# An attention and FFN sandwich on one core: another order of the first quads

## The chip, the cores and the metric

The kernel runs on one core of one Trainium2 chip. The metric is the device time of one execution in microseconds (us). The kernel before was executed three times: 944.52, 944.43 and 942.95 us, median 944.43. A further execution, under the hardware profiler, took 944.22 us, with a span of 942.4 us; all rows here come from it. The difference of 1.8 us between the two lies outside the first and the last instruction.

## The reference, cut to what matters

Four sequences of 1024 rows with 128 channels go through self-attention with 16 heads of 8 channels. Each head's weights are applied to the whole 128-channel input, and the 16 results are projected back to 128 channels by a 2048x128 matrix. A small mixing FFN follows. Layer norms stand before and after each half.

```python
def _L0_attn_ref(x, weight):
    y = x.reshape(b, t, nh, hs).transpose(0, 2, 1, 3)
    scores = jnp.einsum('bhtk,bhsk->bhts', y, y) / math.sqrt(hs)
    attn = jax.nn.softmax(scores, axis=-1)
    o = jnp.einsum('bhts,bsc->bhtc', attn, x)
    o = o.transpose(0, 2, 1, 3).reshape(b, t, nh * c)
    return o @ weight
...
x = x + _layernorm(_L0_attn_ref(_layernorm(x, axis=-1), L0_attn_weight), axis=-1)
x = x + _layernorm(_L0_ffn_ref(_layernorm(x, axis=-1), ...), axis=-1)
```

## The kernel before

**Steps and quads.** The work is cut into 128 steps. A step j is one head of one row of 512 queries (8 rows, 16 heads). A step has two quads, k = 2j and 2j+1; a quad is four blocks of 128 keys against the 512 queries. One quad passes through five engines:

- `score(k)`, line 552, PE (TensorE): four matmuls into the four banks of `ps_s`. It waits until ACT (ScalarE) has read the quad before it (`weighed`), since there is one `ps_s`, and for the operands `op_s` and `op_t` (ring of four steps, `OP_RING`).
- `weigh(k)`, line 733, ACT: the exponential, 128x2048, into `e_f` (ring of four, so it waits for `split` of quad k-4).
- `cast(k)`, line 409: a DMA from the POOL (GpSimd) queue that rounds `e_f` to float16 in `e_hi`. Quad 0 alone is rounded on DVE (VectorE), `round_first`, line 1074.
- `split_quad(k)`, line 1110, DVE: `e_lo` = `e_f` - `e_hi`. It waits for the cast.
- `products(k)`, lines 571 to 573, PE: twelve matmuls, for each of four blocks y_hi x e_hi, y_hi x e_lo, y_lo x e_hi, summed over the step's two quads in `ps_o`. It waits for `split` of its quad. An even quad also waits for `o_split` of the step two before, which frees its half of `ps_o`.

A step ends with `take_o(j)` (ACT, line 738) and `split_o(j)` (DVE, line 1116), which bring the sum to two float16 tiles; `project(j)` (PE, lines 586 to 588, twelve short matmuls into `ps_r`), `invert(j)` (DVE, line 1122), `scale(j)` (ACT, line 745, four instructions, after which `ps_r` is free for the next `project`), `add(j)` (DVE, line 1132).

**The order.** Each engine runs a program written out by hand, a loop over k; nothing is scheduled by a tool. PE does score(k), then products(k-4) (`LAG` = 4), then in some iterations a projection. `step_at(k, lead)` says which step is projected, inverted, scaled or added in iteration k: steps 0 and 1 in the two iterations lead+2 and lead+3, later ones in every second iteration. PE projects with lead 8, ACT and DVE follow with leads 9 and 10.

**The opening.** Before the loop the input is normalised, and the operands of steps 0 to 3 are made on the chip. Those of step 4 onward come through scratch tensors in DRAM: SP (SyncE) writes `yT` and `shT` to `scr_s` and `scr_t` (lines 291 to 302) and loads them back, `load_s` (line 314) and `load_t` (line 321), four DMAs each. The projection's weights are prepared inside the loop: `weight_columns` and sixteen `weight_base` on DVE (lines 1079 and 1082), `square_weights` on ACT (line 805), `weight_sum` on PE, `weight_scale` (eight tiny instructions, lines 1088 to 1094), `weights_high` (ACT, line 752), `weights_neg` (ACT, line 758), `weights_low` (DVE, line 1100). `turn_ffn_weights` (PE, line 538) turns the FFN's weights. The FFN and the norms of a row, and the normalisation of the next sequence, run in pieces between the quads of later rows.

Of the kernel before, what the change touches and what calls it, by code (L numbers as in the profile page):

```python
# [12 lines left out]
P = 128  # L13
# [9 lines left out]
OP_RING = 4  # L23
SPAN = 42
# [6 lines left out]
def sandwich(nc, x, weight, w_r, w_k, w_v, mu_r, mu_k, out):  # L31
# [22 lines left out]
    with ctx:  # L54
# [63 lines left out]
        o_hi = sb("o_hi", [P, 2, BANK], F16)  # L118
        o_neg = sb("o_neg", [P, 2, BANK], F16)
# [22 lines left out]
        l_mid = sb("l_mid", [P, 2, RB, C], F32)  # L142
# [118 lines left out]
        def op_loaded(j):  # L261

            return 128 * (j // OP_RING + 1 - (j % OP_RING < FIRST))

# [5 lines left out]
        def _(sp):  # L270
# [57 lines left out]
            for j in (FIRST, FIRST + 1):  # L328
                load_t(j)
# [33 lines left out]
        def _(pool):  # L363
# [75 lines left out]
            for k in range(LAST):  # L439
                if 0 < k < QUADS:  # L440
                    cast(k)
# [16 lines left out]
        def _(pe):  # L458
# [97 lines left out]
            def products(k):  # L556
                j, q = k // 2, k % 2
                b, ring = batch_of(j), k % EH_RING
                pe.wait_ge(split, k + 1)
# [9 lines left out]
                for g in range(4):  # L569
# [5 lines left out]
                mm.then_inc(product, 1)  # L575

            def project(j):
# [6 lines left out]
                for i in range(RB):  # L584
                    dst, here = ps_r[:, i * P:(i + 1) * P], slice(i * P, (i + 1) * P)
                    nc.tensor.matmul(dst, o_hi[:, j % 2, here], w_hi[:, j % H, :], start=True, stop=False)  # L586
                    nc.tensor.matmul(dst, o_hi[:, j % 2, here], w_lo[:, j % H, :], start=False, stop=False)  # L587
                    mm = nc.tensor.matmul(dst, o_neg[:, j % 2, here], w_neg[:, j % H, :], start=False, stop=True)  # L588
# [29 lines left out]
            for k in range(LAST):  # L618
                if k < QUADS:
                    score(k)  # L620
# [35 lines left out]
            def last_project(u):  # L656
                pe.wait_ge(l_split, u + 1)
                for i in range(PAIR):
                    here = slice(WIDE * u + i * P, WIDE * u + (i + 1) * P)
                    dst = half_ps("project", u)[:, i * P:(i + 1) * P]  # L660
                    nc.tensor.matmul(dst, o_hi[:, LAST_STEP % 2, here], w_hi[:, H - 1, :], start=True, stop=False)
                    nc.tensor.matmul(dst, o_hi[:, LAST_STEP % 2, here], w_lo[:, H - 1, :], start=False, stop=False)
                    mm = nc.tensor.matmul(dst, o_neg[:, LAST_STEP % 2, here], w_neg[:, H - 1, :], start=False, stop=True)
# [49 lines left out]
        def _(act):  # L713
# [21 lines left out]
            def take_o(j):  # L735
                act.wait_ge(product, 2 * j + 2)
                ge(act, projected, j - 1)
                nc.scalar.activation(o_hi[:, j % 2, :], ps_o[:, j % 2, :], ACT.Copy,  # L738
# [109 lines left out]
            for k in range(LAST):  # L848
# [16 lines left out]
                if k == 8:  # L865
                    weights_high()
                if k == 9:
# [554 lines left out]
```

## Time and profile before

| what | value |
|---|---|
| median of three executions | 944.43 us |
| profiled execution, its own time | 944.22 us |
| its span | 942.4 us |
| PE busy (matmul) | 911.7 us, 97% |
| DVE busy | 863.3 us, 92% |
| ACT busy | 755.6 us, 80% |
| POOL busy | 214.3 us, 23% |
| PE in the chain that ended last | 88% |
| DMA engines busy, POOL's cast queue | 73.7% |
| DMA engines busy, SP's queue | 15.3% |

A busy share is a mean over all stages. A matmul's record is longer than its turn on the engine (a 512-column matmul is recorded with 0.38 us and the next one starts 0.22 us after it), so a busy PE may still have small gaps, and durations in a chain are read from start to start. Idle time of an engine that nobody waits for costs nothing.

### The profile page before, as it was taken

The page shows a single profiled execution, that of the slowest core. Times are in us where ns is not written, and L with a number is a line of the kernel's source. Part 1 is how long each engine was busy: PE and PEld are TensorE (multiplying, and loading weights), DVE is VectorE, ACT ScalarE, POOL GpSimd, SP SyncE. Part 2 cuts the span into 40 slices and gives each one's busy share as a digit, 9 for nine tenths or more (in the row PEclk, how much of TensorE's full clock was granted, in tenths as well). Part 3 has the DMA queues.
Part 4 walks back from the last instruction along what each step waited for, and adds up shares of the span by engine and source line. Part 5 has one row for each costly group of instructions (what it writes and reads, how often), then busy time and mean ns, then how long its engine had stood idle before and what let it go on. Part 6 is the DMA issues. An engine that isn't in the chain of part 4 may idle for free.

```text
span 942.4 us, 17739 instructions
## 1 busy us (share of the span) xinstructions
PE 911.7 (97%) x6057; PEld 441.9 (47%) x6057; DVE 863.3 (92%) x1206; ACT 755.6 (80%) x1052; POOL 214.3 (23%) x345
## 2 busy tenths in 40 slices
PE   4889999999999999999999999999999999999996
PEld 2344444454444444444444454544454444544453
DVE  7888898999899999989989999999989998999976
ACT  7778778788879778888778888888878887788855
POOL 2111322221131412213113333222113131132110
PEclk9999999999999999999999999999999999999998
DMA  8999999999899988999889998999989998899830
GB/s 223 193 207 192 214 194 201 221 199 194 179 182 193 188 176 175 210 189 223 181 180 190 192 189 161 185 222 214 191 179 183 196 187 177 175 184 199 163 67 24
DMA packets 100762, 174.17 MB, mean 185 GB/s; under 512 B 21056, under 2 KB 63424, under 8 KB 100672
## 3 DMA queue, kind: packets, MB, share of 16 engines
q0 software_dynamic: 36720, 133.71, 73.7%
q1 hardware_dynamic: 63952, 39.32, 15.3%
q8 instruction: 49, 0.80, 0.3%
q14 instruction: 41, 0.34, 0.1%
HBM read 28.77 MB, written 10.49 MB: 42 GB/s over the span
## 4 chain that ended last, share of the span: by engine, by line
PE 88%; issue 3%; DVE 3%; DMA 2%; ACT 2%; SPq 1%; POOL 1%; POOLq 0%; DVEq 0%; ACTq 0%
PE ps_o L571 24%; PE ps_o L573 22%; PE ps_o L572 22%; PE ps_s L552 8%; PE ps_r L586 3%; PE ps_r L587 3%; PE ps_r L588 3%; DMA e_hi<-e_f 1%; SPq L314 1%; PE ps_x L603 1%; ACT e_f L733 1%; PE ps_x L613 1%; PE ps_x L609 1%; DMA scr_s<-yT 1%; DMA op_t<-scr_t 1%
## 5 line engine op out<-in xcount | busy, mean ns | idle before, releaser
L1110 DVE TENSOR_TENSOR e_lo<-e_f,e_hi 128x2048 f16<-128x2048 f32 x256 | 585.1, 2287 | 37.3 <-DMA e_hi<-e_f 36.7
L733 ACT ACTIVATE e_f<-ps_s 128x2048 f32<-128x2048 f32 x256 | 481.2, 1880 | 150.7 <-PE ps_s L552 141.3
L571 PE MATMUL ps_o<-e_hi,y_hi 128*128 128x512 f16 x1024 | 391.8, 383 | 0.7 <-DVE e_lo L1110 0.5
L573 PE MATMUL ps_o<-e_hi,y_lo 128*128 128x512 f16 x1024 | 389.2, 380 | 0.0
L572 PE MATMUL ps_o<-e_lo,y_hi 128*128 128x512 f16 x1024 | 389.1, 380 | 0.0
L409 POOL DMA_DIRECT2D e_hi<-e_f x255 | 137.5, 539 | 676.7 <-ACT e_f L733 602.1
L571 PEld LDWEIGHTS ps_o<-e_hi,y_hi 128*128 128x128 f16 x1024 | 99.8, 97 | 149.8 <-issue 50.2
L573 PEld LDWEIGHTS ps_o<-e_hi,y_lo 128*128 128x128 f16 x1024 | 100.4, 98 | 121.6 <-issue 1.2
L745 ACT ACTIVATE part<-ps_r,rden 128x128 f32<-128x128 f32 x508 | 144.3, 374 | 13.0 <-DVE rden L1122 12.7
L572 PEld LDWEIGHTS ps_o<-e_lo,y_hi 128*128 128x128 f16 x1024 | 100.5, 98 | 91.8 <-issue 1.4
L552 PE MATMUL ps_s<-op_t,op_s 32*128 32x512 f16 x1024 | 102.5, 388 | 5.4 <-ACT e_f L733 2.9
L586 PE MATMUL ps_r<-w_hi,o_hi 128*128 128x128 f16 x508 | 91.6, 219 | 2.9 <-ACT part L745 2.9
L1132 DVE TENSOR_TENSOR acc<-acc,part 128x512 f32<-128x512 f32 x119 | 83.2, 699 | 12.0 <-ACT part L745 11.7
L587 PE MATMUL ps_r<-w_lo,o_hi 128*128 128x128 f16 x508 | 91.6, 219 | 0.0
L588 PE MATMUL ps_r<-w_neg,o_neg 128*128 128x128 f16 x508 | 91.6, 219 | 0.0
L1116 DVE SCALAR_TENSOR_TENSOR o_neg<-o_hi,ps_o 128x512 f16<-128x512 f16 x127 | 86.2, 679 | 4.0 <-ACT o_hi L738 4.0
L738 ACT ACTIVATE o_hi<-ps_o 128x512 f16<-128x512 f32 x127 | 75.6, 595 | 2.2 <-PE ps_o L573 1.3
L552 PEld LDWEIGHTS ps_s<-op_t,op_s 32*128 32x128 f16 x1024 | 26.5, 91 | 67.9 <-issue 48.4
L586 PEld LDWEIGHTS ps_r<-w_hi,o_hi 128*128 128x128 f16 x508 | 49.7, 98 | 18.3 <-DVE o_neg L1116 2.5
L587 PEld LDWEIGHTS ps_r<-w_lo,o_hi 128*128 128x128 f16 x508 | 49.7, 98 | 14.7
L588 PEld LDWEIGHTS ps_r<-w_neg,o_neg 128*128 128x128 f16 x508 | 49.7, 98 | 0.0
L1122 DVE RECIPROCAL rden<-ps_r 128x4 f32<-128x4 f32 x127 | 22.6, 178 | 5.5 <-PE ps_r L588 5.5
(228 smaller groups left out, 415.7 us busy)
## 6 DMA issues: line engine op xcount, KB each, us to landing
e_hi<-e_f POOLq DMA_DIRECT2D x255, 512.0 KB, 5.0
op_t<-scr_t SPq DMA_DIRECT2D x496, 32.0 KB, 3.7
op_s<-scr_s SPq DMA_DIRECT2D x496, 16.0 KB, 3.3
scr_s<-yT SPq DMA_DIRECT2D x12, 256.0 KB, 4.6
scr_t<-yT SPq DMA_DIRECT2D x12, 256.0 KB, 4.7
out_dram<-res SPq DMA_DIRECT2D x7, 256.0 KB, 4.6
xs<-in_L_attn_x_dram SPq DMA_DIRECT2D x3, 512.0 KB, 6.5
w_last<-in_L_attn_weight_dram SPq DMA_DIRECT2D x1, 1024.0 KB, 12.3
```

Of the source, the lines that this page charges most:

```text
L409: nc.gpsimd.dma_start(flat(e_hi[:, ring]), flat(e_f[:, k % EF_RING])).then_inc(cast_in[ring], 16)
L552: mm = nc.tensor.matmul(ps_s[:, g, :], op_s[here, slot, q * P:(q + 1) * P], op_t[here, slot, :], start=True, stop=True)
L571: nc.tensor.matmul(dst, y_hi[:, b % 2, s, :], e_hi[:, ring, g, :], start=(q == 0 and g == 0), stop=False)
L572: nc.tensor.matmul(dst, y_hi[:, b % 2, s, :], e_lo[:, ring, g, :], start=False, stop=False)
L573: mm = nc.tensor.matmul(dst, y_lo[:, b % 2, s, :], e_hi[:, ring, g, :], start=False, stop=(q == 1 and g == 3))
L586: nc.tensor.matmul(dst, o_hi[:, j % 2, here], w_hi[:, j % H, :], start=True, stop=False)
L587: nc.tensor.matmul(dst, o_hi[:, j % 2, here], w_lo[:, j % H, :], start=False, stop=False)
L588: mm = nc.tensor.matmul(dst, o_neg[:, j % 2, here], w_neg[:, j % H, :], start=False, stop=True)
L733: nc.scalar.activation(e_f[:, k % EF_RING], ps_s[:], ACT.Exp, scale=1.0 / ROOT).then_inc(weighed, 1)
L745: ins = nc.scalar.activation(part[:, j % 2, i, :], ps_r[:, i * P:(i + 1) * P], ACT.Identity, scale=rden[:, j % 2, i:i + 1])
L1110: dve.tensor_tensor(flat(e_lo[:, ring]), flat(e_f[:, k % EF_RING]), flat(e_hi[:, ring]), ALU.subtract).then_inc(split, 1)
L1116: dve.scalar_tensor_tensor(out=o_neg[:, j % 2, :], in0=o_hi[:, j % 2, :], scalar=2.0 ** O_BITS, in1=ps_o[:, j % 2, :], op0=ALU.mult, op1=A ...
```

## The change

`EARLY`: the first four steps, not the first two, are projected in consecutive iterations, and these are lead+4 to lead+7. `O_RING`: `o_hi` and `o_neg` have four slots, not two. `ROUNDED`: DVE rounds quads 0 and 1, and the DMA cast of quad 1 is gone. `HIGH_FIRST`: in quads 0 to 11 the eight matmuls on `e_hi` come first, on the cast alone, and the four on `e_lo` last, behind `split`. The products of quad 1 are parted around score(5). SP loads s and t of step 4 before s and t of step 5. Weight preparation moves one or two iterations later, the turning of the FFN weights from iteration 12 to 20. ACT does `scale` ahead of `take_o`. `l_mid`, a tile of the last row, now lies in `w_raw`, which is free by then.

```diff
+O_RING = 4
+EARLY = 4
+ROUNDED = 2
+HIGH_FIRST = 12
...
-        l_mid = sb("l_mid", [P, 2, RB, C], F32)
+        l_mid = w_raw[:].rearrange("p (n k) c -> p n k c", n=2)[:, :, 0:RB, :]
...
-            if k in (lead + 2, lead + 3):
-                return k - lead - 2
-            return (k - lead) // 2 if k > lead + 3 and (k - lead) % 2 == 0 else None
+            if lead + EARLY <= k < lead + 2 * EARLY:
+                return k - lead - EARLY
+            return (k - lead) // 2 if k >= lead + 2 * EARLY and (k - lead) % 2 == 0 else None
...
             for j in (FIRST, FIRST + 1):
                 load_s(j)
-            for j in (FIRST, FIRST + 1):
                 load_t(j)
...
-                if 0 < k < QUADS:
+                if ROUNDED <= k < QUADS:
                     cast(k)
...
-            def products(k):
+            def products(k, groups=range(4)):
                 j, q = k // 2, k % 2
                 b, ring = batch_of(j), k % EH_RING
-                pe.wait_ge(split, k + 1)
+                if k >= HIGH_FIRST:
+                    pe.wait_ge(split, k + 1)
+                elif k < ROUNDED:
+                    pe.wait_ge(rounded, k + 1)
+                else:
+                    pe.wait_ge(cast_in[ring], cast_count(k))
...
+                if k < HIGH_FIRST:
+                    for g in range(4) if groups[0] == 0 else ():
+                        s = 2 * g + q
+                        nc.tensor.matmul(dst, y_hi[:, b % 2, s, :], e_hi[:, ring, g, :], start=(q == 0 and g == 0), stop=False)
+                        nc.tensor.matmul(dst, y_lo[:, b % 2, s, :], e_hi[:, ring, g, :], start=False, stop=False)
+                    if groups[-1] == 3:
+                        pe.wait_ge(split, k + 1)
+                        for g in range(4):
+                            mm = nc.tensor.matmul(dst, y_hi[:, b % 2, 2 * g + q, :], e_lo[:, ring, g, :], start=False,
+                                                  stop=(q == 1 and g == 3))
+                        mm.then_inc(product, 1)
+                    return
...
             for k in range(LAST):
+                if k == LAG + 1:
+                    products(1, range(2))
                 if k < QUADS:
                     score(k)
...
-                if 1 <= k - LAG < QUADS:
+                if k == LAG + 1:
+                    products(1, range(2, 4))
+                if 2 <= k - LAG < QUADS:
                     products(k - LAG)
...
-                if k == 12:
+                if k == 20:
                     turn_ffn_weights()
...
-                ge(act, projected, j - 1)
+                ge(act, projected, j - O_RING + 1)
...
-                if k == 8:
+                if k == 9:
                     weights_high()
-                if k == 9:
+                if k == 10:
                     weights_neg()
...
                 if k == 2:
+                    round_quad(1)
+                if k == 3:
                     weight_columns()
...
-                if k == 6:
+                if k == 7:
                     weight_scale()
-                if k == 8:
+                if k == 10:
                     weights_low()
```

The order on PE from score(4) to score(6), before (lines of the kernel before; 552 is the score, 571 to 573 the products):

```order
L552 MATMUL ps_s<-op_t,op_s 128x512 [waits weighed,first_t_in,first_s_in]
L552 MATMUL ps_s<-op_t,op_s 128x512 x3
L552 MATMUL ps_s<-op_t,op_s 128x512 [waits weighed]
L552 MATMUL ps_s<-op_t,op_s 128x512 x3
L571 MATMUL ps_o<-e_hi,y_hi 128x512 [waits split]
L572 MATMUL ps_o<-e_lo,y_hi 128x512
L573 MATMUL ps_o<-e_hi,y_lo 128x512
```

and with the change (559 is the score, 584 and 585 the products on `e_hi`, 589 those on `e_lo`):

```order
L559 MATMUL ps_s<-op_t,op_s 128x512 [waits weighed,first_t_in,first_s_in]
L559 MATMUL ps_s<-op_t,op_s 128x512 x3
L584 MATMUL ps_o<-e_hi,y_hi 128x512 [waits rounded]
L585 MATMUL ps_o<-e_hi,y_lo 128x512
L559 MATMUL ps_s<-op_t,op_s 128x512 [waits weighed]
L559 MATMUL ps_s<-op_t,op_s 128x512 x3
L589 MATMUL ps_o<-e_lo,y_hi 128x512 [waits split,rounded]
L589 MATMUL ps_o<-e_lo,y_hi 128x512 x3
```

The eight products of quad 1 on `e_hi` (the pair of rows comes four times) now stand between score(4) and score(5) and wait for a rounding on DVE; the four on `e_lo` follow score(5).

The order on DVE from the first `split_quad` on, before (1110 is `split_quad`, 1079 and 1082 the weights' columns and bases):

```order
L1110 TENSOR_TENSOR e_lo<-e_f,e_hi 128x2048 [waits rounded]
L1079 TENSOR_TENSOR w_col<-w_raw,w_last 128x16 [waits w_last_in,w_in]
L1082 SCALAR_TENSOR_TENSOR xs<-w_raw,w_col,w_last 128x127 [waits dve_step]
L1082 SCALAR_TENSOR_TENSOR xs<-w_raw,w_col,w_last 128x127 x7
L1110 TENSOR_TENSOR e_lo<-e_f,e_hi 128x2048 [waits cast_in_1]
L1082 SCALAR_TENSOR_TENSOR xs<-w_raw,w_col,w_last 128x127 x4
L1110 TENSOR_TENSOR e_lo<-e_f,e_hi 128x2048 [waits cast_in_2]
```

and with the change (1139 is `split_quad`, 1103 `round_quad`, 1108 and 1111 the columns and bases):

```order
L1139 TENSOR_TENSOR e_lo<-e_f,e_hi 128x2048 [waits rounded]
L1103 CAST e_hi<-e_f 128x2048 [waits weighed]
L1139 TENSOR_TENSOR e_lo<-e_f,e_hi 128x2048 [waits rounded]
L1108 TENSOR_TENSOR w_col<-w_raw,w_last 128x16 [waits w_last_in,w_in]
L1111 SCALAR_TENSOR_TENSOR xs<-w_raw,w_col,w_last 128x127 [waits dve_step]
L1111 SCALAR_TENSOR_TENSOR xs<-w_raw,w_col,w_last 128x127 x7
L1139 TENSOR_TENSOR e_lo<-e_f,e_hi 128x2048 [waits cast_in_2]
L1111 SCALAR_TENSOR_TENSOR xs<-w_raw,w_col,w_last 128x127 x4
```

The rounding of quad 1 is new on DVE, and the split of quad 1 now stands ahead of the weights' columns and bases and waits for no DMA.

## Rows read from the trace of the kernel before

**Rows 1.** Waits of PE from 20 to 75 us: in total, times, longest

```profile
PE ps_r L586 <- ACT part L745: 2.9, 2, 2.2
PE ps_s L552 <- DMA op_t<-scr_t: 2.2, 1, 2.2
PE ps_s L552 <- ACT e_f L733: 2.0, 1, 2.0
```

**Rows 2.** Waits of PE from 75 to 915 us

```profile
PE ps_o L571 <- DVE o_neg L1116: 0.2, 1, 0.2
```

**Rows 3.** Timeline of PE: start, duration, line and operation [idle before, releaser]

```profile
26.92 0.40 PE L552 MATMUL ps_s<-op_t,op_s 32*128 32x512 f16 x4 [1.98 <-ACT e_f L733]
...
43.71 0.39 PE L552 MATMUL ps_s<-op_t,op_s 32*128 32x512 f16 x4
...
46.73 0.39 PE L552 MATMUL ps_s<-op_t,op_s 32*128 32x512 f16 x4
...
50.42 0.39 PE L552 MATMUL ps_s<-op_t,op_s 32*128 32x512 f16 x4
...
57.82 0.49 PE L538 MATMUL ps_x<-ident,wf 128*128 128x128 f32 x3
...
74.75 0.39 PE L552 MATMUL ps_s<-op_t,op_s 32*128 32x512 f16 x4
```

**Rows 4.** A stretch: from and to, length, busy PE, PEld, DVE, ACT, POOL (instructions), PEclk, DMA share, GB/s

```profile
39.60:42.90 3.30, 3.30 (x10) 1.13 (x9) 3.07 (x2) 3.30 (x2) 0.53 (x1) 0.51 0.53 111
```

**Rows 5.** Timeline of ACT

```profile
27.37 1.88 ACT L733 ACTIVATE e_f<-ps_s 128x2048 f32<-128x2048 f32 x1 [0.50 <-PE ps_s L552]
29.14 1.90 ACT L805 ACTIVATE w_neg<-w_raw 128x2048 f16<-128x2048 f32 x1
...
31.03 1.87 ACT L733 ACTIVATE e_f<-ps_s 128x2048 f32<-128x2048 f32 x1
...
33.81 0.59 ACT L738 ACTIVATE o_hi<-ps_o 128x512 f16<-128x512 f32 x1
...
41.22 1.98 ACT L752 ACTIVATE w_hi<-xs,ws 128x2032 f16<-128x2032 f32 x1
...
52.84 1.14 ACT L745 ACTIVATE part<-ps_r,rden 128x128 f32<-128x128 f32 x4
```

**Rows 6.** Timeline of DVE

```profile
14.15 1.23 DVE L1074 CAST e_hi<-e_f 128x2048 f16<-128x2048 f32 x1
...
18.19 2.28 DVE L1110 TENSOR_TENSOR e_lo<-e_f,e_hi 128x2048 f16<-128x2048 f32 x1
20.39 0.19 DVE L1079 TENSOR_TENSOR w_col<-w_raw,w_last 128x16 f32<-128x16 f32 x1
20.62 2.18 DVE L1082 SCALAR_TENSOR_TENSOR xs<-w_raw,w_col,w_last 128x127 f32<-128x127 f32 x8
...
36.14 0.15 DVE L1088 TENSOR_SCALAR w_bits<-w_sum 128x1 f32<-128x1 f32 x1
...
37.58 0.69 DVE L1116 SCALAR_TENSOR_TENSOR o_neg<-o_hi,ps_o 128x512 f16<-128x512 f16 x1
...
43.23 2.34 DVE L1100 SCALAR_TENSOR_TENSOR w_lo<-xs,ws,w_hi 128x2032 f16<-128x2032 f32 x1 [0.56 <-ACT w_hi L752]
```

**Rows 7.** Timeline of POOL's and SP's DMA issues

```profile
17.60 0.78 POOL L409 DMA_DIRECT2D e_hi<-e_f  x1 [1.31 <-ACT e_f L733]
20.28 0.53 POOL L409 DMA_DIRECT2D e_hi<-e_f  x1 [1.91 <-ACT e_f L733]
...
24.27 7.10 SPq L314 DMA_DIRECT2D op_s<-scr_s  x8
31.42 6.42 SPq L321 DMA_DIRECT2D op_t<-scr_t  x8
```

**Rows 8.** DMA issue at 17.60 us: size, us to landing

```profile
e_hi<-e_f POOLq DMA_DIRECT2D x1, 512.0 KB, 6.4
```

**Rows 9.** DMA queues over the span: packets, MB, share of the 16 engines

```profile
q0 software_dynamic: 36720, 133.71, 73.7%
```

More of the change, by code:

```diff
@@ L568, in products @@
                 dst = ps_o[:, j % 2, :]
-                for g in range(4):
+                if k < HIGH_FIRST:
[10 more added lines that the diff above has]
+                    return
+                for g in groups:
                     s = 2 * g + q
@@ L736, in take_o @@
                 act.wait_ge(product, 2 * j + 2)
-                ge(act, projected, j - 1)
-                nc.scalar.activation(o_hi[:, j % 2, :], ps_o[:, j % 2, :], ACT.Copy,
+                ge(act, projected, j - O_RING + 1)
+                nc.scalar.activation(o_hi[:, j % O_RING, :], ps_o[:, j % 2, :], ACT.Copy,
                                      scale=2.0 ** -O_BITS).then_inc(taken, 1)
@@ L864, in _ @@
                     keep_weight_sum()
-                if k == 8:
+                if k == 9:
                     weights_high()
-                if k == 9:
+                if k == 10:
                     weights_neg()
-                if k == 12:
+                if k == 20:
                     turn_in_ffn_weights()
+                j = step_at(k, LAG + 5)
+                if j is not None and j < LAST_STEP - 1:
+                    scale(j)
                 j = (k - LAG - 2) // 2
@@ L873, in _ @@
                     take_o(j)
-                j = step_at(k, LAG + 5)
-                if j is not None and j < LAST_STEP - 1:
-                    scale(j)
                 for r, o in rows_at(k):
@@ L892, in last_take @@
                 act.wait_ge(projected, LAST_STEP - 1)
-                nc.scalar.activation(o_hi[:, LAST_STEP % 2, :], ps_o[:, LAST_STEP % 2, :], ACT.Copy,
+                nc.scalar.activation(o_hi[:, LAST_STEP % O_RING, :], ps_o[:, LAST_STEP % 2, :], ACT.Copy,
                                      scale=2.0 ** -O_BITS).then_inc(l_taken, 1)
@@ L1114, in split_o @@
                 dve.wait_ge(taken, j + 1)
-                ge(dve, projected, j - 1)
-                dve.scalar_tensor_tensor(out=o_neg[:, j % 2, :], in0=o_hi[:, j % 2, :], scalar=2.0 ** O_BITS,
+                ge(dve, projected, j - O_RING + 1)
+                dve.scalar_tensor_tensor(out=o_neg[:, j % O_RING, :], in0=o_hi[:, j % O_RING, :], scalar=2.0 ** O_BITS,
                                          in1=ps_o[:, j % 2, :], op0=ALU.mult, op1=ALU.subtract).then_inc(o_split, 1)
@@ L1288, in last_split @@
                 dve.wait_ge(projected, LAST_STEP - 1)
-                dve.scalar_tensor_tensor(out=o_neg[:, LAST_STEP % 2, wide(u)], in0=o_hi[:, LAST_STEP % 2, wide(u)],
+                dve.scalar_tensor_tensor(out=o_neg[:, LAST_STEP % O_RING, wide(u)], in0=o_hi[:, LAST_STEP % O_RING, wide(u)],
                                          scalar=2.0 ** O_BITS, in1=ps_o[:, LAST_STEP % 2, wide(u)], op0=ALU.mult,
```

39 lines of the change are left out of this document (21 added, 18 removed).

## The prediction

> **What bounds the kernel now.** I read the waits of PE first. From 75 to 915 us PE, the engine of the matmuls, waits for 0.2 us in all [rows 2]: the middle is PE's own work, and a start that is x us earlier ends x us earlier. Two quads and a projection take 3.02 and 3.69 us from score to score (43.71 to 46.73 to 50.42) [rows 3], 6.71 together. From 20 to 75 us PE waits 7.1 us in the rows shown: 2.0 for the exponential before score(5), 2.2 for the operand `op_t` of score(8), 2.9 in two waits for `scale` before projections [rows 1]. From 39.60 to 42.90 us the granted clock is 0.51, thus 1.2 GHz in place of 2.4, though PE is busy throughout; that cost 3.3 x 0.49 = 1.6 us [rows 4]. The change touches this stretch and nothing behind it but `l_mid`, which only changes an address. So the sum is the start of score(17): 74.75 us before [rows 3]. By then five projections have run in both kernels.
>
> **The units.** Start to start, a weighing takes 1.77 (27.37 to 29.14), the next score can start after about 1.93 (its record of 1.88 and a hand-over), and a weighing starts 0.45 after its score (26.92 to 27.37) [rows 3, 5]. A score and its products hold PE 3.02, the score 0.33 of it; a projection 0.7. On ACT: squares or `weights_neg` 1.85, `weights_high` 1.9, `take_o` 0.5, `scale` 1.14, so that with its hand-over the next projection can start some 1.28 after scale's start [rows 5]. On DVE: split 2.2, rounding 1.23, columns 0.23, eight bases 2.1 (four: 1.05), the weight scale 37.58 - 36.14 = 1.45, `split_o` 0.6, `weights_low` 2.25 [rows 6]; for two batch sums I allow 0.4.
>
> **DVE with the change.** The first split starts at 18.19 as before; the rounding of quad 1 follows at 20.4 and its split ends at 23.85, columns and bases at 26.2. Split(2) needs cast(2), issued at 20.28. In the trace the first cast took 6.4 us to land [rows 8]; cast(2) now stands first in its queue, so I take 6.4 again, 26.7. Lower bound 2.7, the bare work of a cast (73.7% of 942.4 us over 255 casts [rows 9]); then the bases at 26.2 set the split. Upper bound 9.1, as if 2.7 more still stood ahead of it. From 26.7: split(2) to 28.9, bases 29.95, split(3) 32.15, bases 33.2, split(4) 35.4, split_o(0) 36.0, split(5) 38.2, weight scale 39.65, split(6) 41.85, split_o(1) 42.45, split(7) 44.65, split(8) 46.85, `weights_low` 49.1, split_o(2) 49.7, split(9) 51.9, split(10) 54.1, sums 54.5, split_o(3) 55.1, invert(0) 55.3.
>
> **PE and ACT with the change.** Score(5) starts at 26.92 as before, because weigh(4) sets it. But the eight products of quad 1 now fill the 2 us ahead of it; the four on `e_lo` end at 28.1. Score(6) then waits for weigh(5) alone, 27.37 + 1.93 = 29.3. ACT does weigh(5), the squares and weigh(6) at 31.03, unchanged [rows 5], so score(7) comes at 32.95. Weigh(7) starts at 33.4, products(3) end at 36.0.
> Score(8) follows at 36.0 if `op_t` of step 4 is there. SP issued its eight s loads from 24.27 and the eight t loads from 31.42 to 37.84 [rows 7]. Now t of step 4 is issued after four s loads, from about 28 to 31.5 us; before, its last DMA left at about 34.6, halfway through the eight, and score(8) came at about 39.1 (43.71 - 3.02 - 1.6). So it arrives about 3 us earlier, at 36.0 or before. The wait of 2.2 us goes, and I take the slow clock to go with it.
> Score(9) 39.05, weigh(9) 39.5. Then ACT becomes the slow one: `weights_high` 41.25, weigh(10) 43.1, `weights_neg` 44.9, take_o(2) 46.7, weigh(11) 47.2. PE: score(10) 42.05, score(11) 45.2, products(7) end 48.15, score(12) waits for weigh(11) until 49.1. Products(8) need split_o(2), 49.8. They end at 52.4; project(0) has its weights (49.1) and ends at 53.15; score(13) 53.2, before at 61.3 (74.75 less two pairs of 6.71). So 8 us are gained here. The four projections in a row give part back: each waits for the scale of the step before, and scale follows a weighing on ACT, a round of 0.75 + 0.45 + 1.77 + 1.28 = 4.25 us against PE's own 3.69. Scale(0) at 55.4, project(1) 56.7, and then 60.95, 65.2 and 69.45; score(17) at 70.2. That is 4.55 earlier. The turning of the FFN weights, in a wait before (57.82 [rows 3]), now stands in PE's full stretch: 0.4 lost. **Gain 4.15 us**, 944.22 - 4.15 = 940.1. The profiled execution is 0.2 below the median of 944.43.
>
> **Edits that I cost at nothing.** Products on `e_hi` first, in quads 2 to 11: in the chain above each split is done before the four late matmuls and nearly always before the first, so only quad 1 profits; cover gone, it would save up to a split of 2.2 us once. The same matmuls in another order, each with its own weight load: no count changes. `O_RING` = 4: it lets `take_o` run ahead of late projections; without it take_o(2) would wait for project(0). The missing cast(1): 2.7 us of the DMA engines; it shows only in the landing of cast(2). DMA load: casts 2 to 9 are issued from 20.3 to 41.4, 8 x 2.7 = 21.6 us of work plus an estimated 4 of loads and scratch writes, done by about 46; cast(9) is needed at 49.7, so they fit, by an estimated 1 to 4 us each.
> POOL's cast of 17.60 lasted 0.78 us, that of 20.28 0.53 [rows 7]; the longer one began while DVE was on its copies for the shift. A rounding on DVE will now run at 20.4, right behind the issue of cast(2). I give this nothing beyond the landing of 6.4. The Trainium skill, "SBUF — State Buffer", section "SBUF: two separate sides", warns against just this: an fp32 copy on VectorE locks GpSimd out while it should write the descriptors of its DMA. By that rule cast(2) would land up to one rounding, 1.2 us, later; the sum would give 941.0 or so. The row of 0.78 fits it, by 0.25 us only.
>
> **The rivals.**
> *More gain, 936 to 938.5.* If scale keeps up, its four waits of 0.56 go, and DVE's 0.5 us behind cast(2) with them: 940.1 - 2.7 = 937.4. For it: after 75 us PE has 0.2 us of waits [rows 2]. Against: there one projection per two quads leaves room; here four come in a row. Chance 0.13.
> *Late casts, 942.* If casts 6 to 8 land 2 us later than taken, DVE, without slack from split(2) to split_o(2), passes it on through products(8): 942.1. For it: more and larger transfers start in 20 to 41 us than PE's waits for the operand suggest there is room for [rows 1]. Against: the sum of work above. Chance 0.13, half of it within 0.2% of no change.
> *One fall of the clock, 941.7.* PE still waits about 1 us before score(6) and before score(12). Before, the 0.51 came behind the wait of 2.2 us [rows 1, 4]; one fall costs 1.6. Chance 0.06. The Trainium skill, "TensorE: Matmul & The Clock Gate", section "Part 1: The HAM clock gate", says that idleness throttles the array; the trace agrees at 39.6.
> *Slower, by the clock.* The same at every new pause (before scores 6, 7 and 12 and in the row of projections, 1 us or less each): four falls cost 6.4, 946.5. It decides from four on; with three the time is 944.9. Against: the longest new pause is half of the 2.2 us. Chance 0.04.
> *It does not do what it says.* If `op_t` of step 4 comes no earlier, because t must wait for the shift's scratch write, score(8) stays at 39.1 and little is left: 943.5 to 944.4. Against: the write is issued ahead of all these loads, and the s loads alone take until 28 [rows 7]. Chance 0.04.
>
> **The numbers.** Forecast 940.1, chance 0.60, own range 938.5 to 941.8. The range is 936.9 to 942.9, which takes in more gain and late casts. A measurement can tell 0.2%, 1.9 us, from no change: faster means below 942.5. Faster: 0.60 + 0.13 + half of 0.13 + 0.06 = 0.85. Same: the other half and the last rival, 0.11. Slower: 0.04.
>
> **What would show it.** In the profile after: score(8) near 36 us without a wait for `op_t`; granted clock 1.0 from 23 us on; score(12) near 49 behind an exponential; project(1) to (4) each waiting about 0.5 us for `part`; score(17) near 70.2; no wait of PE from 75 to 910 us. It is wrong if DVE waits for casts 6 to 8, if a fall of the clock appears after 23 us, or if score(17) comes at 72 or later.

## The result and the profile after

The changed kernel took 940.17 us (median of 7 executions, 938.80 to 941.35), the kernel before, on the same chip and in turn with it, 943.65 us (7 executions, 942.95 to 944.52). The ratio is 0.996, 95% interval 0.9949 to 0.9971: faster by 0.4%, twice what a measurement can tell. The profiled execution took 939.56 us with a span of 937.8 us, 4.66 us less than before's 944.22. PE is busy for 908.8 us, DVE 864.3, ACT 756.1, POOL 212.9; the shares are as before, so the time must be read from the opening.

The waits of PE from 20 to 72 us in the kernel after (in total, times, longest), to be held against [rows 1]:

```profile
PE ps_s L559 <- ACT e_f L762: 2.2, 3, 1.1
PE ps_r L611 <- ACT part L774: 1.7, 4, 0.4
PE ps_s L559 <- issue: 0.7, 1, 0.7
PE ps_o L584 <- DVE o_neg L1145: 0.6, 2, 0.4
```

The wait for `op_t` is gone. The two waits for `part`, one of them 2.2 us long, are now four of 0.4. The waits for an exponential are shorter and more: 1.1 before score(6), 0.4 before score(7), 0.7 before score(12).

The timeline of PE, to be held against [rows 3] (start, duration, line, operation [idle before, releaser]); L559 is the score, L584 a product on `e_hi`, L589 one on `e_lo`, L595 the first kind of product from quad 12 on:

```profile
26.85 0.39 PE L559 MATMUL ps_s<-op_t,op_s 32*128 32x512 f16 x4
27.18 1.04 PE L589 MATMUL ps_o<-e_lo,y_hi 128*128 128x512 f16 x4
29.32 0.40 PE L559 MATMUL ps_s<-op_t,op_s 32*128 32x512 f16 x4 [1.11 <-ACT e_f L762]
...
35.91 0.40 PE L559 MATMUL ps_s<-op_t,op_s 32*128 32x512 f16 x4
...
49.10 0.40 PE L559 MATMUL ps_s<-op_t,op_s 32*128 32x512 f16 x4 [0.70 <-ACT e_f L762]
...
49.87 0.38 PE L584 MATMUL ps_o<-e_hi,y_hi 128*128 128x512 f16 x1 [0.37 <-DVE o_neg L1145]
...
53.22 0.39 PE L559 MATMUL ps_s<-op_t,op_s 32*128 32x512 f16 x4
...
70.28 0.40 PE L559 MATMUL ps_s<-op_t,op_s 32*128 32x512 f16 x4
...
405.90 0.38 PE L595 MATMUL ps_o<-e_hi,y_hi 128*128 128x512 f16 x1 [0.76 <-DVE o_neg L1145]
...
895.89 0.40 PE L559 MATMUL ps_s<-op_t,op_s 32*128 32x512 f16 x4
```

These are score(5), the late products of quad 1, score(6), score(8), score(12), products(8), score(13), score(17), a product near 406 us, and the last score. Beside the forecast:

| start of score | before | forecast | after |
|---|---|---|---|
| 5 | 26.92 | 26.92 | 26.85 |
| 6 | | 29.3 | 29.32 |
| 8 | 39.00 | 36.0 | 35.91 |
| 10 | 46.73 | 42.05 | 41.96 |
| 12 | 54.89 | 49.1 | 49.10 |
| 13 | 61.32 | 53.2 | 53.22 |
| 17 | 74.75 | 70.2 | 70.28 |

Scores 14, 15 and 16 start at 57.49, 61.75 and 66.02, a round of 4.27 us where 4.25 was worked out. The gain is 8.1 us at score(13) and 4.5 at score(17).

The windows of after (from and to, length, busy PE, PEld, DVE, ACT, POOL, PEclk, DMA share, GB/s), the first to be held against [rows 4], and then the second window in the kernel before:

```profile
39.60:42.90 3.30, 3.03 (x18) 1.17 (x16) 3.30 (x3) 3.30 (x2) 0.53 (x1) 1.00 1.00 195
928.00:933.00 5.00, 2.70 (x18) 2.02 (x16) 4.11 (x15) 3.76 (x10) 0.00 (x0) 1.00 0.18 52
```

```profile
928.00:933.00 5.00, 3.26 (x12) 2.52 (x13) 3.35 (x9) 4.01 (x11) 0.00 (x0) 0.75 0.00 0
```

From 39.60 to 42.90 the granted clock is now 1.00 where it was 0.51. From 928 to 933 it is 1.00 where it was 0.75.

**Where the 4.66 us are.** At score(17) the gain is 4.47. Turning the FFN weights costs 0.34 of it (score(20) to score(21) takes 4.03 us where that pair of quads takes 3.69), which leaves 4.13. The last score came at 899.42 us in the timeline of before and comes at 895.89 now: 3.53, so 0.6 is lost on the way. The wait of 0.76 us at 405.90 accounts for it: just ahead of it the gain is 4.35 us (a score at 404.74 that stood at 409.09; before had lost 0.2 in its own wait [rows 2]), behind it 3.53 (409.70 against 413.23). The last score to the end of the span takes 41.91 us where it took 42.98. These 1.07 us come from a stretch in which the change moves only the address of `l_mid`, and in which the clock fell once where it fell twice before. In all fourteen traces the tail takes 41.63 to 41.91 us with one fall in it (eight of them, runs 3 and 6 with the old `l_mid` too) and 42.75 to 43.69 with two (six). So what goes with the longer tail is the second fall, not `l_mid`. The medians, 3.5 us apart, fit the 3.53 of the last score.

The wait at 405.90 is for `o_neg` from DVE. DVE's timeline of after (before: [rows 6]) has, besides quad 1's rounding and split(2), the split which was late there:

```profile
20.32 1.22 DVE L1103 CAST e_hi<-e_f 128x2048 f16<-128x2048 f32 x1
...
26.65 2.29 DVE L1139 TENSOR_TENSOR e_lo<-e_f,e_hi 128x2048 f16<-128x2048 f32 x1 [0.46 <-DMA e_hi<-e_f]
...
49.05 0.68 DVE L1145 SCALAR_TENSOR_TENSOR o_neg<-o_hi,ps_o 128x512 f16<-128x512 f16 x1
...
398.67 2.29 DVE L1139 TENSOR_TENSOR e_lo<-e_f,e_hi 128x2048 f16<-128x2048 f32 x1 [1.60 <-DMA e_hi<-e_f]
```

The split at 398.67 waited 1.60 us for a cast to land; before, the longest such wait near it was 0.67 us, at 401.59. DVE had not made this up by 405.90. The DMA share around it is the same in both traces (1.06 from 390 to 400 us), so why this cast was later is open. The changed kernel's second trace (run 9) has a wait for `o_neg` of only 0.3 us between 390 and 420 us, so its size is not a property of the kernel.

The issues of POOL and SP in after, against [rows 7], and then the landing of cast(2), against [rows 8]:

```profile
20.20 1.47 POOL L416 DMA_DIRECT2D e_hi<-e_f  x1 [3.99 <-ACT e_f L762]
...
21.42 3.81 SPq L322 DMA_DIRECT2D op_s<-scr_s  x4
25.28 3.30 SPq L329 DMA_DIRECT2D op_t<-scr_t  x4
```

```profile
e_hi<-e_f POOLq DMA_DIRECT2D x1, 512.0 KB, 6.4
```

Cast(2) landed in 6.4 us, as taken. Its record on POOL was 1.47 us long instead of 0.53. SP's loads began at 21.42, 2.9 us earlier than before, which was not forecast. What SP waited for ahead of its s loads reads, from 18 to 34 us, first before, then after:

```profile
SPq L309 <- DMA scr_s<-yT: 3.0, 1, 3.0
```

```profile
SPq L317 <- DMA scr_s<-yT: 0.2, 1, 0.2
```

It is the last of the scratch writes of `yT` to `scr_s`: issued at 18.23 before, it landed 6.0 us later; without cast(1) beside it, issued at 18.15, it landed in 3.2 us. The shift's write to `scr_t`, which only the t loads need, landed in 3.2 us instead of 7.7 (issued at 20.83 and 20.92); in neither of the two kernels did SP have to wait for it, since the s loads took longer.

### The profile page after: what moved, and what is told of

Read it like the earlier page. It is cut to its first block, busy times and chain, and to the rows that moved or that the text cites. A ratio compares the mean times of both kernels' runs of the same rounds, so it can differ in the third digit from the quotient of the medians.

```text
span 937.8 us, 17735 instructions
## 1 busy us (share of the span) xinstructions
PE 908.8 (97%) x6057; PEld 439.8 (47%) x6057; DVE 864.3 (92%) x1207; ACT 756.1 (81%) x1052; POOL 212.9 (23%) x344
## 4 chain that ended last, share of the span: by engine, by line
PE 88%; DVE 5%; issue 2%; ACT 2%; DMA 2%; POOL 0%; POOLq 0%; DVEq 0%; ACTq 0%
PE ps_o L595 24%; PE ps_o L597 22%; PE ps_o L596 22%; PE ps_s L559 8%; PE ps_r L611 3%; PE ps_r L612 3%; PE ps_r L613 3%; DVE e_lo L1139 2%; DMA e_hi<-e_f 2%; ACT e_f L762 1%; PE ps_x L628 1%; PE ps_x L638 1%; PE ps_x L634 1%; ACT part L774 0%; PE ps_x L623 0%
## 5 line engine op out<-in xcount | busy, mean ns | idle before, releaser
L595 PE MATMUL ps_o<-e_hi,y_hi 128*128 128x512 f16 x976 | 372.3, 381 | 0.8 <-DVE o_neg L1145 0.8
L597 PE MATMUL ps_o<-e_hi,y_lo 128*128 128x512 f16 x976 | 369.9, 379 | 0.0
L596 PE MATMUL ps_o<-e_lo,y_hi 128*128 128x512 f16 x976 | 369.9, 379 | 0.0
L595 PEld LDWEIGHTS ps_o<-e_hi,y_hi 128*128 128x128 f16 x976 | 94.9, 97 | 142.0 <-issue 46.4
L597 PEld LDWEIGHTS ps_o<-e_hi,y_lo 128*128 128x128 f16 x976 | 95.5, 98 | 115.3
L596 PEld LDWEIGHTS ps_o<-e_lo,y_hi 128*128 128x128 f16 x976 | 95.6, 98 | 86.9 <-issue 0.3
L559 PE MATMUL ps_s<-op_t,op_s 32*128 32x512 f16 x1024 | 102.6, 388 | 4.3 <-ACT e_f L762 3.1
L559 PEld LDWEIGHTS ps_s<-op_t,op_s 32*128 32x128 f16 x1024 | 26.5, 91 | 67.0 <-issue 49.8
L1151 DVE RECIPROCAL rden<-ps_r 128x4 f32<-128x4 f32 x127 | 22.3, 175 | 5.2 <-PE ps_r L613 5.2
```

Source lines behind the costliest of these rows:

```text
L559: mm = nc.tensor.matmul(ps_s[:, g, :], op_s[here, slot, q * P:(q + 1) * P], op_t[here, slot, :], start=True, stop=True)
L595: nc.tensor.matmul(dst, y_hi[:, b % 2, s, :], e_hi[:, ring, g, :], start=(q == 0 and g == 0), stop=False)
L596: nc.tensor.matmul(dst, y_hi[:, b % 2, s, :], e_lo[:, ring, g, :], start=False, stop=False)
L597: mm = nc.tensor.matmul(dst, y_lo[:, b % 2, s, :], e_hi[:, ring, g, :], start=False, stop=(q == 1 and g == 3))
```

## The experiments

The open questions were which of the edits bring the 4.5 us at score(17), whether the slow stretch hung on the wait for `op_t`, whether the longer record on POOL costs anything, and what the row of four late projections gives back. Each run was compared with the kernel before on the same chip; its median was 943.36 us beside the first four, 944.28 beside the next four and 943.09 beside the last four. The changed kernel is 3.5 us faster than it in the result and 3.1 in run 9, so between groups a difference of medians is good to some tenths of a us only, and the starts of the scores say more.

**1. Products in the old order.** In the changed kernel:

```
-HIGH_FIRST = 12
+HIGH_FIRST = 0
```

> The changed kernel with HIGH_FIRST = 0: in quads 2 to 11 the twelve products go back to the old order and wait for the split; quad 1 stays parted around score(5), now six and six. Theory (the splits are always done before PE comes to the products): no difference from the changed kernel, 940.2, within 0.5 us, score(17) again at 70.3 us in the trace. Rival (products that start on the rounded values alone are what lets PE start earlier): 1.5 us or more slower than the changed kernel, with waits of PE for e_lo.

Measured 941.04 us, ratio 0.997 (0.996 to 0.9979). PE's timeline, score(4) and score(17):

```profile
24.75 0.40 PE L559 MATMUL ps_s<-op_t,op_s 32*128 32x512 f16 x4 [0.29 <-issue]
...
70.55 0.39 PE L559 MATMUL ps_s<-op_t,op_s 32*128 32x512 f16 x4
```

Both are 0.28 us later than in after (24.47 and 70.28), so from one to the other the two kernels run alike, and no product waits for `e_lo`. Products on `e_hi` first are worth nothing here. The 0.9 us between the medians do not come from the opening: the last score starts at 896.01 us against 895.89 in after, and of the 2.0 us between the two profiled executions 1.8 lie in the tail, where the clock fell twice in this run.

**2. Quad 1 cast by DMA again.** In the changed kernel, with the weights' columns and bases back in their earlier iterations:

```
-ROUNDED = 2
+ROUNDED = 1
...
-                if k == 2:
-                    round_quad(1)
-                if k == 3:
+                if k == 2:
                     weight_columns()
```

> The changed kernel with quad 1 rounded by the DMA again (ROUNDED = 1) and the weights' columns and bases back in iterations 2 to 4 on DVE. Theory (DVE's chain up to split_o(2) sets products(8)): the rounding costs DVE 1.2 us but saves 2.3 us of waits for casts, so split_o(2) ends at 50.4, not 49.7, and score(17) comes 0.7 us later: 940.9. SP's loads of step 4 start at 24.3 again, not 21.4, and still arrive by 36. Rival (the cast taken from the DMA engines is the main gain, through earlier operands and casts): 2.5 us or more slower than the changed kernel, 942.7, with a wait for op_t at score(8).

Measured 941.1 us, ratio 0.9973 (0.9964 to 0.9983). Score(17) starts at 71.66, 1.4 us later than in after, where 0.7 was expected. At score(13) it is 1.0 us (54.18 against 53.22), which split_o(2) explains; the rest comes at score(14), which waits 0.37 us for `op_t` in this run and not at all in after. The timeline of DVE shows quad 1's split behind its cast, and split_o(2) later than the 49.05 of after:

```profile
24.20 2.29 DVE L1139 TENSOR_TENSOR e_lo<-e_f,e_hi 128x2048 f16<-128x2048 f32 x1 [1.35 <-DMA e_hi<-e_f]
...
50.00 0.68 DVE L1145 SCALAR_TENSOR_TENSOR o_neg<-o_hi,ps_o 128x512 f16<-128x512 f16 x1
```

The rounding on DVE more than pays for itself: it takes 1.2 us of DVE's time, but without it a split waits 1.35 us for the cast, and PE waits twice for `op_t` (0.30 us ahead of score(10), 0.37 ahead of score(14)).

**3. The load order alone.** In the kernel before:

```
             for j in (FIRST, FIRST + 1):
                 load_s(j)
-            for j in (FIRST, FIRST + 1):
                 load_t(j)
```

> The kernel before with one edit: SP issues s4, t4, s5, t5 in place of s4, s5, t4, t5. Theory (each cure of the operand wait works, but the early projections take back most of it): the wait of 2.15 us at score(8) goes, score(10) comes 3.4 us earlier, and then products(6) wait for split_o(1), which stands behind weights_low on DVE; 1.5 us faster than before in the end, 942.1. If the clock falls in that wait instead, 943.6. Rival (the operand wait and its slow clock are worth their full 3.8 us): 939.9.

Measured 941.59 us, ratio 0.9979 (0.997 to 0.9989). PE's timeline, score(8) and score(17), and its wait for `o_neg` from 20 to 72 us:

```profile
36.92 0.40 PE L551 MATMUL ps_s<-op_t,op_s 32*128 32x512 f16 x4
...
73.50 0.40 PE L551 MATMUL ps_s<-op_t,op_s 32*128 32x512 f16 x4
```

```profile
PE ps_o L570 <- DVE o_neg L1115: 2.4, 2, 1.2
```

Score(8) no longer waits, as forecast. But a new wait of 2.4 us for `o_neg` takes the place of the old one: what was late next is DVE, whose weights stand ahead of `split_o`. At score(17) 1.25 of the 2.1 us won at score(8) are left.

**4. The rounding alone.** In the kernel before, `cast(1)` is left to DVE, which rounds quad 1 ahead of the weights' columns:

```
-                if 0 < k < QUADS:
+                if 1 < k < QUADS:
                     cast(k)
...
                 if k == 2:
+                    round_quad(1)
                     weight_columns()
```

> The kernel before with one edit: quad 1 rounded on DVE (in iteration 2, ahead of the weights' columns) and its cast taken from the DMA queue; order of SP's loads unchanged. Theory (removing the cast lets the scratch writes land 3 us earlier, so SP starts at 21.4 and t of step 4 arrives by 36 even in the old order): the same as the edit of the load order, 1.5 us faster than before, 942.1, no wait for op_t at score(8). Rival (only the load order cures the wait): op_t is waited for at score(8) as before and the time is 943.7 or, with 1.2 us more on DVE, 944.5.

Measured 941.64 us, ratio 0.9981 (0.9971 to 0.9992). The issues of SP's loads in this run and, in PE's timeline, score(8):

```profile
21.90 5.97 SPq L314 DMA_DIRECT2D op_s<-scr_s  x8
27.91 6.00 SPq L321 DMA_DIRECT2D op_t<-scr_t  x8
```

```profile
37.58 0.40 PE L552 MATMUL ps_s<-op_t,op_s 32*128 32x512 f16 x4
```

The loads keep their old order and still start at 21.90 instead of 24.27, and score(8) doesn't wait for `op_t`. So the wait had two cures, and the change applies both: the order of the loads, and one cast fewer among the transfers ahead of them. Each alone brings about 1.8 us (943.36 less 941.59 and 941.64), and run 5, which has both, brings 1.6: they do not add up. This run also moved the slow stretch (see the section on the hardware).

**5. Projections, ring and weights as before.** In the changed kernel:

```
-O_RING = 4
-EARLY = 4
+O_RING = 2
+EARLY = 2
...
-                if k == 9:
+                if k == 8:
                     weights_high()
-                if k == 10:
+                if k == 9:
                     weights_neg()
...
-                if k == 7:
+                if k == 6:
                     weight_scale()
-                if k == 10:
+                if k == 8:
                     weights_low()
```

with the turning at 12 and `take_o` ahead of `scale`, as before.

> The changed kernel with EARLY = 2, O_RING = 2, and the weights, the turning of the FFN weights and the order of take_o and scale as before; the opening (rounding, load order, high first, quad 1 parted) is kept. Theory: products(6) wait about 2 us for split_o(1) behind weights_low, score(12) at 52.7, score(13) at 59.2 against 53.2 in the changed kernel and 61.3 before; in the end 2.2 us faster than before, 941.4, so the later projections are worth the other 1.3 to 2. Rival (the opening alone is the gain): as the changed kernel, 940.2.

Measured 942.72 us, ratio 0.9986 (0.9975 to 0.9998). Its timeline of PE, scores 12, 13 and 17, and its waits from 20 to 72 us:

```profile
52.72 0.39 PE L559 MATMUL ps_s<-op_t,op_s 32*128 32x512 f16 x4
...
59.16 0.39 PE L559 MATMUL ps_s<-op_t,op_s 32*128 32x512 f16 x4
...
74.28 0.40 PE L559 MATMUL ps_s<-op_t,op_s 32*128 32x512 f16 x4
```

```profile
PE ps_r L611 <- ACT part L774: 2.9, 2, 2.3
PE ps_o L584 <- DVE o_neg L1145: 2.3, 2, 1.2
```

Scores 12 and 13 were expected at 52.7 and 59.2. The wait of 2.3 us for `part` and that for `o_neg` are back. So later projections with a deeper ring, and weights that keep out of the way of `split_o`, carry somewhat more than half. Against the kernel before on its own chip this run is 1.6 us faster and the change 3.5, which leaves 1.9 for them. At score(13) they are worth 5.9 us; at score(17) 4.0, of which 1.7 are the slow stretch between scores 13 and 14 of this run (see the section on the hardware), so 2.3. What each of these edits is worth by itself was not run.

**6. PE kept busy in the wait for `op_t`.** In the kernel before, ten matmuls of 512 columns, whose product nobody reads, stand ahead of score(8):

```
+            def fill(n):
+                pe.wait_ge(w_summed, 1)
+                for _ in range(n):
+                    nc.tensor.matmul(ps_x[:], ident16[:], y_hi[:, 0, 0:RB, :]...,
+                                     start=True, stop=True)
...
+                if k == 8:
+                    fill(10)
```

> The kernel before with ten matmuls of 512 columns into the idle ps_x ahead of score(8), where PE waits 2.15 us for op_t; the wait is filled, not shortened, and the results do not change. Theory (the stretch at half the clock comes from that pause): granted clock 1.0 from 37 to 43 us, score(9) 3.0 us after score(8) in place of 4.7, 1.6 us faster than before, 942.0. Rival (the fall has another cause, or its loss is hidden by ACT): the same as before, 943.65.

This failed: 946.19 us, ratio 1.0025 (1.0009 to 1.0041), slower. PE's timeline and two windows of this run:

```profile
36.64 2.32 PE L620 MATMUL ps_x<-y_hi,ident 128*128 128x512 f16 x10
...
39.25 0.39 PE L552 MATMUL ps_s<-op_t,op_s 32*128 32x512 f16 x4 [0.29 <-DMA op_t<-scr_t]
...
60.05 0.22 PE L586 MATMUL ps_r<-w_hi,o_hi 128*128 128x128 f16 x1 [2.25 <-ACT part L753]
...
60.82 0.39 PE L552 MATMUL ps_s<-op_t,op_s 32*128 32x512 f16 x4
...
65.53 0.39 PE L552 MATMUL ps_s<-op_t,op_s 32*128 32x512 f16 x4
```

```profile
39.60:42.90 3.30, 3.30 (x22) 1.35 (x19) 3.04 (x2) 3.20 (x2) 0.53 (x1) 1.00 0.50 103
60.80:65.50 4.70, 4.70 (x18) 1.59 (x16) 4.58 (x7) 2.91 (x5) 0.53 (x1) 0.64 0.57 146
```

The clock does stay at 1.00 from 39.60 to 42.90, as expected. But score(13) starts at 60.82, only 0.5 us ahead of before's 61.32. Counted from score(8), which came 0.25 us later here, 0.75 us are won: of the 1.7 us which the slow stretch cost PE (4.71 us from score(8) to score(9) where it is 3.02 here), 0.9 were hidden behind other engines that were late anyway; score(10) now waits 0.49 us for its exponential. And the clock falls in the quad behind score(13) instead, which takes 4.71 us where it took 3.02; PE had come out of its next long pause, 2.25 us for `part`, at 60.05. There nothing hides the fall. So with the filler the fall stands behind another pause; this is one trace of each kernel, and whether every execution falls there is not shown. The span is 1.0 us longer than before's; the rest of the 1.9 us between the medians stays open.

**7. Projections 1 to 3 between score and products.** In the changed kernel:

```
                     first_operands(1)
...
+                    if k - LAG - 9 in (1, 2, 3):
+                        project(k - LAG - 9)
                     products(k - LAG)
...
-                if j is not None and j < LAST_STEP:
+                if j is not None and j < LAST_STEP and j not in (1, 2, 3):
                     project(j)
```

> The changed kernel with projections 1, 2 and 3 moved one iteration on, between the score and the products of quads 14, 15 and 16. Theory (in the catch-up the round weigh, scale, project of 4.25 us sets the pace because the projection stands ahead of the next score): the next score no longer waits for the scale, score(17) at 68.3 in place of 70.3, 2.0 us faster than the changed kernel, 938.2. Rival (another engine limits there, DVE or the casts): within 0.5 us of the changed kernel.

Measured 938.7 us (937.2 to 938.84), ratio 0.9937 (0.9924 to 0.995). PE's timeline:

```profile
68.63 0.39 PE L559 MATMUL ps_s<-op_t,op_s 32*128 32x512 f16 x4
```

Score(17) starts 1.65 us earlier than in after, though its opening began 0.6 us later (score(4) at 25.07 against 24.47), and no projection waits for `part`. So the round of 4.27 us was what the row of four projections gave back, and it need not be: each score stood behind a waiting projection for no reason of its own data.

**8. The same, and DVE's and ACT's weights moved further.** On top of 7, `weights_neg` in iteration 11, `weights_low` in iteration 11 behind split_o(2), and the batch sums of the next sequence three iterations later.

> As the kernel with the moved projections, and weights_neg from iteration 10 to 11 on ACT, weights_low from 10 to 11 on DVE behind split_o(2), and the batch sums of sequence 1 from iterations 12 and 13 to 15 and 16. Theory (score(12) waits for ACT and products(8) for split_o(2)): score(12) at 48.3, products(8) at 48.7, score(17) at 67.7; 2.6 us faster than the changed kernel, 937.6. Rival (what is gained at score(12) is lost again at project(1)): as the kernel with the moved projections alone, 938.2.

Measured 938.71 us, ratio 0.994 (0.9928 to 0.9952), no better than 7. Score(12) starts at 48.48 instead of 49.10 in after and 49.70 in run 7, but project(1) then waits 1.0 us for `part` and a score 0.5 us for `op_t`, and score(17) is at 68.71.

**9. The changed kernel again,** as the neighbour of the last three runs.

> The changed kernel once more, on the same chip as the next three. Both theories: 0.3 to 0.5% under the kernel before. It is there to compare the next three with.

Measured 939.99 us (939.05 to 941.75), ratio 0.9967 (0.9955 to 0.9979): the result repeats, with score(17) at 70.25.

**10. The rounding ahead of the first split.** In the changed kernel, so that DVE's copy no longer runs while POOL issues cast(2):

```
+                if k == 2:
+                    round_quad(1)
                 if 0 <= k - 2 < QUADS:
                     split_quad(k - 2)
-                if k == 2:
-                    round_quad(1)
```

> The changed kernel with the rounding of quad 1 ahead of the first split on DVE, so that it ends at 19.4, before POOL issues cast(2) at 20.2. Theory (the rounding holds up POOL while it writes the cast's descriptors): the cast's record falls from 1.47 to 0.53 us, the landing from 6.4 us to 5.5 or less, DVE's wait before split(2) from 0.46 to 0; products(8) and score(17) 0.4 us earlier, 0.4 us faster than the changed kernel. Rival (the longer record is bookkeeping, and the DMA engines, busy with the scratch writes, set the landing): record shorter, but the landing stays at 26.6 us and the time is the same.

Measured 940.62 us, ratio 0.9969 (0.9957 to 0.9981). POOL's issue of cast(2), its landing, and DVE's split(2):

```profile
20.36 0.78 POOL L416 DMA_DIRECT2D e_hi<-e_f  x1 [3.99 <-ACT e_f L762]
```

```profile
e_hi<-e_f POOLq DMA_DIRECT2D x1, 512.0 KB, 6.3
```

```profile
26.65 2.29 DVE L1139 TENSOR_TENSOR e_lo<-e_f,e_hi 128x2048 f16<-128x2048 f32 x1 [0.45 <-DMA e_hi<-e_f]
```

The record shrinks from 1.47 to 0.78 us; the landing goes from 6.4 to 6.3, and split(2) starts at the same 26.65. DVE's copy did lengthen POOL's instruction, and taking it away gains nothing: score(17) starts at 70.58, as late against score(4) as in run 9, and 940.62 is not below the 939.99 of run 9.

The delay was real all the same, and another transfer had the good of it. From 21.6 to 22.5 us the cast's queue moves nothing in after, and in none of the other six traces with the rounding right behind cast(2)'s issue; in this run, 11 and 12 its packets run from 21.6 us on. In exchange the shift's scratch write, issued at 20.8 to 21.1, lands in 2.6 to 3.5 us in those seven traces and in 5.4 to 6.0 in these three. In after, then in this run:

```profile
scr_t<-shT SPq DMA_DIRECT2D x1, 256.0 KB, 3.2
```

```profile
scr_t<-shT SPq DMA_DIRECT2D x1, 256.0 KB, 5.8
```

Here SP then waits 0.9 us for it and starts the t loads of step 4 at 26.82 instead of 25.28; score(8) still does not wait.

**11 and 12. Both improvements with that rounding.** Run 11 is 7 with the edit of 10, run 12 is 8 with it.

> Projections 1 to 3 between score and products, as in the run of that alone, with the early rounding. Theory: the two gains add, 2.0 + 0.4 us, 2.4 us faster than the changed kernel. Rival (DVE's and DMA's stretch near 400 us takes back what PE gains, as there PE waits for o_neg for 0.4 to 1.0 us): 1.5 us or less.

> The version with the moved weights and sums as well, with the early rounding. Theory: score(12) at 48.3 and score(17) at 67.0 without a fall of the clock, 3.2 us faster than the changed kernel. Rival (as before, most of the extra is lost to later waits or to the clock): the same as the version with the moved projections and early rounding, within 0.5 us.

Run 11: 937.77 us (936.96 to 938.09), ratio 0.9938 (0.9926 to 0.9949). Run 12: 937.33 us (936.24 to 938.15), ratio 0.9934 (0.9922 to 0.9946). Score(12) starts at 48.07 in run 12, and PE's timeline has score(17):

```profile
67.49 0.39 PE L559 MATMUL ps_s<-op_t,op_s 32*128 32x512 f16 x4
```

Both beat both kernels: 2.2 and 2.7 us below the changed kernel beside them. The two can't be told apart.

## Why the prediction was right, step by step

- **What bounds the kernel.** Right in kind: PE's work from score(17) to the end sets the time, and the gain there reached the last score. The rule "a start x us earlier ends x us earlier" was off by 0.6 us, through one cast that landed late near 399 us; the forecast sign "no wait of PE from 75 to 910 us" failed with the 0.76 us at 405.90.
- **The chain to score(17).** Each start of the table came within 0.15 us. ACT's `weights_high` and `weights_neg` set score(12); products(8) then waited 0.37 us for split_o(2); the four scales gave the round of 4.27. Run 5 shows how much later projections and weights bring together, and run 7, by taking the four waits for `part` away, that these waits were what held the row back.
- **"The wait of 2.2 us goes."** Right, but for one reason out of two. I named the order of the loads; the missing cast(1) does it as well (runs 3 and 4). My "it shows only in the landing of cast(2)" was the step that failed here: a scratch write to `scr_s` landed in 3.2 us instead of 6.0, and SP's loads, which wait for it, began 2.9 us earlier. It cost the forecast nothing, since score(8) was by then set by PE.
- **"I take the slow clock to go with it."** It went, but that it goes with this wait alone is not what the runs show. Run 6 fills the wait, and there the fall comes some 22 us later, behind the next pause of that length. The change leaves no pause of PE above 1.11 us from 20 to 915, and in the nine profiled executions here of which that holds no opening has a fall. The forecast did not need the 1.6 us from it either: the starts of scores 12 and 13 were built up from ACT's and DVE's work, behind which about half of the slow stretch would have been hidden (0.9 of 1.7 us, run 6).
- **Cast(2) and POOL.** I took 6.4 us for the landing, and it was 6.4. The Trainium skill, "SBUF — State Buffer", section "SBUF: two separate sides", would have had it up to 1.2 us later. The trace agrees with it on the instruction, whose record went from 0.53 to 1.47 us, and back to 0.78 in run 10; in after that record ends at 21.67, just behind the rounding, which ends at 21.54. It does not show the price, since the landing stayed within 0.1 us: the cast's packets started some 0.9 us later, but the shift's scratch write, which otherwise shares the DMA engines with the cast, was then out of the way by about 24 us (run 10). Also the 941.0 which I gave for this case does not follow from my own chain: with no slack from split(2) to products(8), 1.2 us more there make 941.3.
- **The turning.** 0.4 forecast, 0.34 measured.
- **The level.** 940.1 against 940.17 is closer than the working deserves. Against the profiled execution the gain was 4.66, of which 1.07 lie in the tail, where the clock fell once instead of twice. Between the medians it was 3.5, 0.65 less than forecast; the seven executions of before have a median 0.8 us below the 944.43 that I started from, and that made up for it.
- **The rivals.** *Late casts* fell: the casts issued from 33 to 42 us landed in 4.5 to 6.0 us, and DVE waited for none of them. *More gain* fell, because the scales did not keep up; run 7 shows that it takes a different order on PE to get it. *One fall of the clock* and *Slower, by the clock* did not happen in the opening, despite pauses of 1.11 and 0.70 us. *It does not do what it says* fell with the start of score(8).

## What to carry to other kernels

Where an engine works in a fixed order, ask of every instruction that may wait what is queued behind it: taking the weights out of the way of `split_o`, and a ring of four instead of two so that projections can come late, were together worth about 1.9 us, a little more than the 1.6 from curing the wait for the transfer that looked like the bottleneck (run 5), and projecting behind the score instead of ahead of it was worth another 2.2 us (run 11 beside run 9). Two cures for one wait need not add up (runs 3, 4 and 5), so build them one at a time before giving either a price. And before counting a stretch at the slow clock as a gain to be had, see which other engine would be late without it, and whether PE's other long pauses are still there to bring it back.

## What was unexpected in the hardware

**The slow stretch stands behind one pause or another.** Four openings of fourteen have one stretch at the lower clock in the record of the granted clock, each at another place: from 39.6 us before [rows 4], and in runs 4, 5 and 6. In run 4 and in run 5 PE's timeline just ahead of it and the window of it read:

```profile
26.71 0.39 PE L552 MATMUL ps_s<-op_t,op_s 32*128 32x512 f16 x4 [1.98 <-ACT e_f L733]
```

```profile
26.70:31.40 4.70, 4.69 (x16) 1.63 (x16) 4.70 (x8) 3.77 (x3) 1.05 (x2) 0.64 1.05 207
```

```profile
58.39 0.22 PE L611 MATMUL ps_r<-w_hi,o_hi 128*128 128x128 f16 x1 [2.25 <-ACT part L774]
```

```profile
59.20:63.90 4.70, 4.70 (x21) 1.61 (x20) 4.64 (x7) 2.91 (x5) 0.53 (x1) 0.64 0.56 144
```

The mean of 0.64 is a mix of the levels of 1.2 and 2.4 GHz: in run 4 the matmuls of 512 columns follow each other by 0.43 us from 27.5 to 30.5, by 0.22 before and after. The record does not show all of it: ahead of score(4), where it reads 1.00 throughout, such matmuls follow each other by 0.43 us until 22.3 us before and until 23.6 in run 7, and by 0.22 from 21.2 on in after. Run 7's later start of score(4) fits this. A quad takes 4.71 us with such a stretch in it and 3.02 without. All four begin within 1.5 us behind a pause of PE: 2.15 us before, 1.98 in run 4, 2.25 in runs 5 and 6. Five kernels have pauses of 1.98 us or more in the opening, ten pauses in all; four of these were followed by a fall, never two in one opening, and in run 3 neither of its two was. Pauses of up to 1.25 us, in all kernels, were followed by none. The Trainium skill, "TensorE: Matmul & The Clock Gate", section "Part 1: The HAM clock gate", ties falls to idleness of the array; the traces agree in that each of the four came behind a long pause. Which of the long pauses brings one stays open.

**Executions of one kernel differ, and so does their clock.** Over its seven executions the changed kernel had a mean granted clock of 0.995 in those of 940.75 to 941.35 us, and of 0.997 or 0.999 in those of 938.80 to 940.17 (those of 0.997 being the fastest two, so it is not the clock alone). In the profiled executions the tail has part in it, where the clock falls once or twice: before it is low from 930.5 to 934.0 and again from 937.4, in after from 935.9 only, in run 1 from 926.7 to 933.6 and again from 937.0; the second fall goes with 0.8 to 2.1 us (see the result). That this is also what parts the executions of one kernel is not shown, since both traces of the changed kernel have one fall. A difference of 1 us between kernels with the same opening, as between run 1 and the change, is of this size; the starts of the scores in the trace were the better witness.

**A cast holds back other queues.** One 512 KB cast fewer at 17.6 us, and of two 256 KB scratch writes on another queue one landed in 3.2 instead of 6.0 us, the other in 3.2 instead of 7.7. And it matters when the cast's packets start: with the next cast's record 0.7 us shorter they started some 0.9 us earlier, and the second write took 5.4 to 6.0 us (runs 10 to 12).
